# Two-layer graph network, one core: catch-up segments from block rows 12, 16, 24 on, a twelve-block tail, and three reordered steps

## What is computed

```python
def _L0(X, adj, W, b):
    deg = clip(sum(adj, axis=1) + 1.0, 1.0)
    z = concat([X, (adj @ X + X) / deg], axis=1) @ W + b
    out = relu(z);  return out / max(norm(out, axis=1), 1e-12)
def _L1(X, adj, W):
    deg = sum(adj, axis=1)
    return concat([X, adj @ X / (deg + 1.0)], axis=-1) @ W.T
x = layernorm(x + _L0(x, adj, W0, b0))
x = layernorm(x + _L1(x, adj, W1))
```

## Time and profile before

| | us |
|---|---|
| median of three runs | 753.95 (752.53 to 753.97) |
| the profiled execution, its own time | 753.86 |
| its span, first to last instruction | 751.7 |
| around the span | 2.2 |

### The profile page before, as it was taken

One profiled execution on the slowest core, in us unless ns is written; L12 is line 12 of the kernel. 1 busy time (PEld: TensorE's weight loads), 2 busy tenths in 40 slices (PEclk: granted clock), 3 DMA queues, 4 the chain that ended last, 5 costly groups with the idle time before them and its releaser, 6 DMA issues.

```text
span 751.7 us, 27897 instructions
## 1 busy us (share of the span) xinstructions
PE 632.5 (84%) x11125; PEld 579.6 (77%) x11125; DVE 670.9 (89%) x2469; ACT 618.5 (82%) x969; POOL 250.9 (33%) x344
## 2 busy tenths in 40 slices
PE   1467667778787888889899998999999999999995
PEld 0467666667676777778798887999898998989995
DVE  6879899889998998998999998999999999987894
ACT  6788898989998989899899988898998989870143
POOL 0122434333322233324335232535352434321034
PEclk9986988989999999999999999999999999999998
DMA  9999999999999999999999999999999999910002
GB/s 343 420 419 420 421 419 421 418 420 419 419 420 419 401 422 416 410 418 395 420 400 422 417 419 381 407 412 411 413 393 419 396 421 418 415 76 3 2 28 94
DMA packets 41515, 274.54 MB, mean 365 GB/s; under 512 B 4454, under 2 KB 8614, under 8 KB 8614
## 3 DMA queue, kind: packets, MB, share of 16 engines
q1 hardware_dynamic: 41152, 272.65, 88.7%
q10 hardware_dynamic: 230, 0.07, 0.0%
HBM read 270.60 MB, written 2.10 MB: 363 GB/s over the span
## 4 chain that ended last, share of the span: by engine, by line
PE 33%; DMA 23%; DVE 16%; issue 11%; ACT 10%; POOL 4%; SPq 1%; ACTq 0%; DVEq 0%; POOLq 0%
DMA a_in<-in_adj 23%; PE s_ps L388 16%; ACT junk L591 7%; PE u_ps L407 5%; DVE t_sb L812 5%; DVE e L805 4%; POOL small L1177 4%; DVE q_sb L876 2%; PE p_ps L374 2%; DVE y_sb L870 2%; PE s_ps L473 2%; PE u_ps L469 1%; PE z_ps L457 1%; PE p_ps L469 1%; SPq L339 1%
## 5 line engine op out<-in xcount | busy, mean ns | idle before, releaser
L591 ACT ACTIVATE junk<-a_in 128x2048 uint8<-128x2048 uint16 x256 | 488.6, 1912 | 17.7 <-DMA a_in<-in_adj 16.9
L388 PE MATMUL s_ps<-xh,t_sb 128*128 128x129 f16 x4096 | 389.4, 252 | 43.1 <-DVE t_sb L812 39.7
L388 PEld LDWEIGHTS s_ps<-xh,t_sb 128*128 128x128 fp8e4 x4096 | 314.3, 103 | 73.1 <-DVE t_sb L812 44.9
L805 DVE TENSOR_SCALAR e<-a_in 128x2048 uint8<-128x2048 f32 x256 | 312.0, 1225 | 24.4 <-DMA a_in<-in_adj 23.5
L1204 POOL COPY store<-pk 128x32 uint32<-128x32 uint32 (+1 forms) x250 | 151.5, 648 | 285.7 <-ACT pk L600 285.7
L812 DVE TENSOR_SCALAR t_sb<-pk 128x128 uint32<-128x128 uint32 x1024 | 156.3, 224 | 7.3 <-ACT pk L600 6.4
L374 PE MATMUL p_ps<-pow_h,e 128*128 128x16 f16 x2048 | 90.9, 171 | 66.2 <-DVE e L805 65.4
L374 PEld LDWEIGHTS p_ps<-pow_h,e 128*128 128x128 f16 x2048 | 77.8, 99 | 80.7 <-DVE e L805 68.4
L1177 POOL TENSOR_TENSOR small<-small,minus_half 128x4 f32<-128x4 f32 x32 | 70.3, 2196 | 167.9 <-DVE small L862 124.1
L407 PE MATMUL u_ps<-xh,u_sb 128*128 128x64 f16 x2976 | 105.1, 192 | 0.0
L407 PEld LDWEIGHTS u_ps<-xh,u_sb 128*128 128x128 fp8e4 x2976 | 100.1, 97 | 1.2
(11 more groups left out here) (120 smaller groups left out, 467.1 us busy)
## 6 DMA issues: line engine op xcount, KB each, us to landing
a_in<-in_adj SPq DMA_DIRECT2D x256, 1024.0 KB, 11.9
xl<-in_x SPq DMA_DIRECT2D x4, 512.0 KB, 12.8
out_h<-e SPq DMA_DIRECT2D x8, 256.0 KB, 2.5
b_sb<-in_L_gnn_b ACTq DMA_DIRECT2D x3, 0.2 KB
w_sb<-in_L_gnn_W ACTq DMA_DIRECT2D x1, 32.0 KB
w_raw<-in_L_gnn_W ACTq DMA_DIRECT2D x1, 32.0 KB
```

What stands on the lines that cost most here:

```text
L388: last = nc.tensor.matmul(s_ps[:, n % 2, at:GW], t_sb[:, b // 2, b % 2::2], xh[:, b, at:GW], start=(b == 0), stop=False)
L591: nc.scalar.activation(junk[:, t % 2, :], halves[t % R], ACT.Copy, scale=1.0 / 128, accum_out=half_sum[:, n, c:c + 1]).then_inc(s_half, 1)
L805: nc.vector.tensor_scalar(e8[:, c, :], a_in[:, t % R, :], 1.0, float(CODE), ALU.is_equal, ALU.add).then_inc(s_e, 1)
```

## The change

`START` is 0, 12, 16, 24, 32, 40, 48, 56. The column blocks below which G is known become 0, 8, 12, 20, 28, 36, 44, 52, and the widths 8, 4, 8, 8, 8, 8, 8 and 12 for the tail. The tail is two passes of six column blocks, with two matmuls of 64 columns for each block in both passes, and one addition in both. There are eight and not six tail buffers. On PE, `transpose_cat(e)` moves ahead of the fourth `pack_chunk` of its row; the wait for the last copy of sums moves behind `dense(e)` in the tail. On ACT, `take_g(e)` moves ahead of `take_packed(n, 0)`. On DVE, `low_part(e)` and `begin_acc(e)` move from the end of row k = 3 to behind the first `compare` of the next row. At the end of the tail the last group is added and squared in two halves.

```diff
-START = [0, 12, 20, 28, 36, 44, 52]
+START = [0, 12, 16, 24, 32, 40, 48, 56]
-W = 8
+LAST = 2 * NB // TG - 1
-VR = 6
+VR = 8
-WIDTH = [W] * (NQ - 1) + [NB - TAIL]
+WIDTH = [low(s + 1) - low(s) for s in range(NQ - 1)] + [NB - TAIL]
+TW = WIDTH[-1] // 2
@@ tail_sums(j) on PE
-                at = TAIL + (j // NV) * W
+                at = TAIL + (j // NV) * TW
                 for r in range(TG):
-                    for b in range(W):
-                        if j < NV:
-                            last = nc.tensor.matmul(v_ps[j % 3][:, r, :], v_sb[:, j % VR, (r * W + b) // 2, b % 2::2],
-                                                    xh[:, at + b, 0:HP], start=(b == 0), stop=(b == W - 1))
-                            continue
+                    for b in range(TW):
                         for part in range(2):
...
+                    if j == LAST and r == TG // 2 - 1:
+                        last.then_inc(s_vps, 1)
@@ PE, the loop over rows
                 for c in range(NC):
-                    pack_chunk(n, c)
                     if e >= 0 and (k, c) == (1, 3):
                         transpose_cat(e)
+                    pack_chunk(n, c)
@@ PE, the tail
-            pe.wait_ge(s_agg, NB)
             pe.wait_ge(s_uadd, NB - START[1])
+            pe.wait_ge(s_glo, (TAIL + TW + BR - 1) // BR)
             tail_sums(0)
             transpose_cat(e)
+            pe.wait_ge(s_pk, NB * 2)
             tail_sums(1)
             dense(e)
+            pe.wait_ge(s_agg, NB)
             tail_sums(2)
@@ ACT
                 sum_codes(n, 2)
-                take_packed(n, 0)
                 if e >= 0 and k == 3:
                     take_g(e)
+                take_packed(n, 0)
@@ DVE, additions of the tail
-                ins = nc.vector.tensor_tensor(rows, v_ps[j % 3][:, :, 0:F], rows, ALU.add)
-                if j < NV:
-                    link(ins)
-                    ins = nc.vector.tensor_tensor(rows, v_ps[j % 3][:, :, F:HP], rows, ALU.add)
-                ins.then_inc(s_vadd, 1)
+                nc.vector.tensor_tensor(rows, v_ps[j % 3][:, :, 0:F], rows, ALU.add).then_inc(s_vadd, 1)
@@ DVE, the loop over rows
                 compare(n, 0)
+                if e >= 1 and k == 0:
+                    low_part(e - 1)
+                    begin_acc(e - 1)
                 if n:
                     unpack(n - 1, 0)
...
-                if e >= 0 and k == 3:
-                    low_part(e)
-                    begin_acc(e)
@@ DVE, the end of the tail
             for g in range(NV):
-                if g:
+                if g == NV - 1:
+                    add_last(0)
                     variance(g - 1)
-                add_tail(NV + g)
-                if g == NV - 1:
+                    square_last(0)
+                    add_last(1)
+                    square_last(1)
                     last_variance()
+                else:
+                    if g:
+                        variance(g - 1)
+                    add_tail(NV + g)
```

More of the change, by code:

```diff
@@ L82, in piece @@
     return j * ROWS[q - 1] // steps, (j + 1) * ROWS[q - 1] // steps
-PIECE = max(piece(n)[1] - piece(n)[0] for n in range(START[1], NB))
+PIECE = max((piece(n)[1] - piece(n)[0]) * WIDTH[seg(n) - 1] for n in range(START[1], NB))
 def turn(slot):
@@ L138, in gnn_kernel @@
         store = sb("store", [P, BASE[NQ]], U32)
-        u_sb = sb("u_sb", [P, PIECE * W // 2, 2 * P], FP8)
+        u_sb = sb("u_sb", [P, PIECE // 2, 2 * P], FP8)
         xh = sb("xh", [P, NB, GW + 1], F16)
@@ L402, in catch_up @@
                         pe.wait_ge(s_uadd, turn(n))
-                half = (r1 - r0 + 1) // 2
+                half, w = (r1 - r0 + 1) // 2, WIDTH[q - 1]
                 for r in (range(half), range(half, r1 - r0))[half_of]:
-                    for b in range(W):
+                    for b in range(w):
                         for part in range(2):
-                            last = nc.tensor.matmul(u_rows[:, r, 0:F], u_sb[:, (r * W + b) // 2, b % 2::2],
+                            last = nc.tensor.matmul(u_rows[:, r, 0:F], u_sb[:, (r * w + b) // 2, b % 2::2],
                                                     xh[:, low(q - 1) + b, part * F:(part + 1) * F],
-                                                    start=(b + part == 0), stop=(b + part == W))
+                                                    start=(b + part == 0), stop=(b + part == w))
                     if r == r1 - r0 - 1:
@@ L464, in tail_sums @@
                     pe.wait_ge(s_vadd, j - 2)
-                at = TAIL + (j // NV) * W
+                at = TAIL + (j // NV) * TW
                 for r in range(TG):
-                    for b in range(W):
-                        if j < NV:
-                            last = nc.tensor.matmul(v_ps[j % 3][:, r, :], v_sb[:, j % VR, (r * W + b) // 2, b % 2::2],
-                                                    xh[:, at + b, 0:HP], start=(b == 0), stop=(b == W - 1))
-                            continue
+                    for b in range(TW):
                         for part in range(2):
-                            last = nc.tensor.matmul(v_ps[j % 3][:, r, 0:F], v_sb[:, j % VR, (r * W + b) // 2, b % 2::2],
+                            last = nc.tensor.matmul(v_ps[j % 3][:, r, 0:F], v_sb[:, j % VR, (r * TW + b) // 2, b % 2::2],
                                                     xh[:, at + b, part * F:(part + 1) * F],
-                                                    start=(b + part == 0), stop=(b + part == W))
+                                                    start=(b + part == 0), stop=(b + part == TW))
+                    if j == LAST and r == TG // 2 - 1:
+                        last.then_inc(s_vps, 1)
                 last.then_inc(s_vps, 1)
@@ L830, in unpack_piece @@
                     dve.wait_ge(s_ups, turn(n))
-                dst = words(u_sb[:, 0:(r1 - r0) * W // 2, :])
+                dst = words(u_sb[:, 0:(r1 - r0) * WIDTH[q - 1] // 2, :])
                 unpack_planes(lambda g: dst[:, :, g * 2 * PKW:(g + 1) * 2 * PKW],
@@ L924, in unpack_tail @@
                 unpack_planes(lambda t: dst[:, :, :, 2 * t * PKW:2 * (t + 1) * PKW],
-                              src[:, :, i * W // 2:(i + 1) * W // 2, :]).then_inc(s_v, 1)
+                              src[:, :, i * TW // 2:(i + 1) * TW // 2, :]).then_inc(s_v, 1)
             def add_tail(j):
@@ L932, in add_tail, with add_last, square_last @@
                 rows = acc[:, (j % NV) * TG:(j % NV + 1) * TG, :]
-                ins = nc.vector.tensor_tensor(rows, v_ps[j % 3][:, :, 0:F], rows, ALU.add)
-                if j < NV:
-                    link(ins)
-                    ins = nc.vector.tensor_tensor(rows, v_ps[j % 3][:, :, F:HP], rows, ALU.add)
-                ins.then_inc(s_vadd, 1)
+                nc.vector.tensor_tensor(rows, v_ps[j % 3][:, :, 0:F], rows, ALU.add).then_inc(s_vadd, 1)
+            def add_last(h):
+                dve.wait_ge(s_vps, LAST + h + 1)
+                dve.wait_ge(s_vadd, LAST)
+                rows = acc[:, NB - TG + h * BR:NB - TG + (h + 1) * BR, :]
+                link(nc.vector.tensor_tensor(rows, v_ps[LAST % 3][:, h * BR:(h + 1) * BR, 0:F], rows, ALU.add))
+            def square_last(h):
+                dve.wait_ge(s_fvar, NV - 4)
+                for n in range(NB - TG + h * BR, NB - TG + (h + 1) * BR):
+                    ins = nc.vector.scalar_tensor_tensor(out=sqf[:, (NV - 1) % 4, n % TG, :], in0=acc[:, n, :], scalar=1.0,
+                                                         in1=acc[:, n, :], op0=ALU.mult, op1=ALU.mult,
+                                                         accum_out=fvar[:, 1, n:n + 1])
+                link(ins)
             def variance(g):
@@ L948, in last_variance @@
                 rows = slice(NB - TG, NB)
[L949 to L955, removed]
                 nc.vector.scalar_tensor_tensor(out=fvar[:, 1, rows], in0=fvar[:, 1, rows], scalar=1.0 / F,
```

## The result

Eleven runs of each kernel gave a median of 755.49 us (754.47 to 756.72) after the change and 753.39 us (752.10 to 754.22) before it. The ratio is 1.0033, with a 95% interval of 1.0025 to 1.0042: slower by 0.33%, 2.1 us. The prediction had 751.5 us and faster as the likeliest; its range up to 757.0 holds the time.

What follows compares the result with a forecast made beforehand. Transfers with a hiccup per group of four were taken to bound rows 12 to 48, PE the rows from 44 on. Span 751.7 + 15.9 - 3.2 - 6.0 - 9.1 = 749.3, with 2.2 around it 751.5 us; range 746.5 to 757.0.

Steps and rivals of the forecast that it cites:

- The reordered steps: Rows 12 to 48: removing ACT's and DVE's waits brings PE to row 48 6.0 us sooner; bounds nothing and 12.1 us.
- g: The time by which PE reaches row 48 sooner; taken as 6.0 us, forecast range 5 to 8.
- 360 us: Rows 12 to 48: what the transfers alone want, at 420 GB/s, where the rows took 372.1 us.
- Near 420 GB/s for 35 of 40 slices: Transfer rate read from the page of the kernel before; it gave 10.0 us a block row, 40 a group of four.
- 757.5 - g: The whole kernel's time in us with the other terms kept and only the gain up to row 48 left open.
- The extra work on PE: Rows 48 to 63 and the last sums: 15.9 us more on PE, less 3.2 of its idle time, +12.7.
- The tail: From the end of the sums to the end: 9.1 us less, bounds 7.5 and 11; 63 us against 72.1 before.
- never made up: Second pass of the tail: `verdict`'s 4.2 us delay stays, as PE's pitch of 2.88 us equals the DVE loop.
- Rival 4: POOL becomes late as copies by `keep` grow from 250 to 285, under 1 us a group: 753 us, chance 0.03.
- Rival 3: Transfers become the only limit up to row 48, g 9.5 to 12, time 745.5 to 748 us; chance 0.16.
- rival 1: Rows 48 to 63: extra work hidden nowhere, reordering gives nothing, g below 2.0, 756 to 757.5 us; chance 0.22.

Runs made afterwards that it cites:

- light catch-ups: Changed kernel without the products with `g_lo` in the catch-ups of rows 48 to 63: 743.15 us in one run.
- ten steps ahead: Against segments of four, ten of `verdict`'s fifteen steps moved into two DVE waits at the head of the tail: 743.34 us.
- segments of four: Changed kernel with segments of four rows from 12 to 56, tail still twelve: 746.48 us, ratio 0.9918 against the kernel before.
- both readers lighter: Changed kernel with ACT's sums and DVE's compare doing half of each chunk from row 12 on, guard flag held at zero: 754.38 us in one run.
- a ring of five: Changed kernel with a ring of five buffers and not six, and six tail buffers and not eight: 756.1 us in one run.
- PE relieved: Changed kernel whose catch-ups of rows 12 to 47 multiply only each row's first block and its high half: 756.15 us in one run.

## Why the prediction was wrong

**The step that failed** is "The reordered steps", where it says "I take half: PE reaches row 48 by g = 6.0 us sooner". It is 1.1 us, about what two runs of the same stream differ by, and the reordering alone gives 0.9 in time. The distance to 360 us, which I took for the upper bound of a gain, was no loss through waits at all: 420 GB/s was read off single slices of the page and taken for the ceiling of a long stretch. "Near 420 GB/s for 35 of 40 slices" was itself read too kindly: 12 of the 35 in the earlier trace rows lie between 343 and 413. And the prediction did not look at DVE's wait for chunks, 12.0 us in 17 waits in the kernel before: an engine that is already waiting for data does not bring the next chunk sooner by being free sooner. Halving both readers' work, and separately leaving out three in ten of PE's matmuls, left row 48's first chunk where it was (503.8 us; 503.9 and 504.1). A wait as large as a loss need not be its cause.

The DMA share in the earlier trace rows, 1.01, is no proof of it by itself. In the changed kernel rows 52 to 55 have a share of 1.00 at 399 GB/s, and there PE sets the pace: it never idles, and DVE waits for a chunk once, for 0.3 us.

**With g = 1.1** and the rest as predicted the formula 757.5 - g gives 756.4. The extra work was 0.7 us less than predicted, the tail gave 0.2 less, and 1.8 and not 2.2 us lie around the span: 755.5, as measured.

**The extra work on PE** was right: 15.9 less 3.2 of idle time makes 12.7, measured 12.0. The groups from row 48 on take 42.1, 42.5, 45.7 and 46.2 where 42, 43, 46 and 46.5 were named, and the light catch-ups confirm that this work sets the time.

**The tail** was right: 63.2 us from the end of the sums against 63, `add_tail(8)` at 34.65 against 34.7, turns of 2.86 against 2.87. PE waits for DVE in the second pass, but only once, 0.32 us at 725.95, since the two pitches are the same (2.88 and 2.86). That `verdict` is never made up there was shown by moving it: the tail is 3.3 us shorter with ten steps ahead (59.8 against 63.1).

**Rival 4** did not come: POOL's 285 copies are hidden, and with segments of four it runs 554 instructions without a loss.

**Rival 3** was half right. The transfers were the limit up to row 48, but at 413 GB/s and already before the change. The range, which reaches 757.0 for rival 1, holds the time, but the forecast, faster with g of 5 to 8, does not. That 755.5 lies inside the range is no support for the mechanism.

## What to carry to other kernels

Before a wait of a reader is priced as a loss, look at whether the same engine also waits for its data in that stretch: here DVE did, 17 times, and removing its other waits moved the idle time to the next chunk and did little more. The DMA share does not tell (1.01 where the transfers set the pace, 1.00 where PE did); a kernel with lighter readers does. Work moved out of a tail is free only where its new place has slack, so count the blocks per group and spread them first (segments of four turned the same tail of twelve from a loss of 2 us into a gain of 6 to 7). In a tail that runs at the pitch of one engine's loop, any step in that loop's engine counts in full, and an earlier wait of the same engine is the place for it.

## What the hardware showed that was not expected

**One of the sixteen transfer streams falls behind, and DVE waits for it.** The trace has sixteen landings for each chunk (the Trainium skill, "DMA: Bandwidth & Descriptors", section "Why a DMA increments its semaphore by 16 and not by 1", says that each transfer engine reports its part; the count agrees). In the changed kernel the last of them is 0.7 us behind the first at row 0, 1.8 at row 4, 2.8 at row 12, 4.7 at row 16, 6.4 at row 24, and 5.2 to 6.9 from there to row 44; at row 36 fifteen lie within 2.6 us and one at 6.5. With both readers lighter, the last is up to 8.9 us behind; with a ring of five it is 3.2 to 4.8 from row 24 to row 44. DVE is released by the last. The last landings hardly move between the kernel before, the changed one and the one with both readers lighter: at row 24 256.8 to 256.9 us, at row 36 380.6 to 380.8, at row 48 503.7 to 503.9 (503.3 to 504.7 in all fourteen kernels). The lag stops growing, and where it stops is the larger the more buffers are free. That fits faster streams that use up the ring and then wait for the slowest, but it is inferred: the records do not name a packet's stream, so neither these waits nor whether it is always the same stream can be seen. So 36 rows take 10.3 us each, while single slices show 420 GB/s. Why one stream falls behind stays open.

**PE's instructions come over the same sixteen streams.** From 136.4 to 508.5 us the changed kernel has 43 packets of 16 KB on queue 8 and 5,509 matmuls, 128 bytes for each matmul with its weight load; with 3,844 matmuls there are 30, again 128 bytes each. (The Trainium skill, "Runtime: NRT & Kernel Launch", section "Instruction fetch mechanics", has 16 KiB blocks that the sequencer fetches itself, mostly hidden; the size agrees.) Where such a packet ends, the records show a data packet that starts there and takes long, where the median of the 8 KB ones is 0.311 us:

```
start us   queue  bytes  us
58.90      8      16384  1.076
59.96      1       8192  0.804
84.98      8      16384  1.098
86.06      1       8192  0.774
111.85     14      8192  0.324
112.16     1       8192  0.968
```

In that stretch a packet of queue 8 takes 0.9 to 1.2 us and one of queue 14 0.31 to 0.55, with up to 0.97 for the data packet behind it. That this is what throws the slowest stream back was the natural story, and for queue 8 the run with PE relieved speaks against it: 13 of 43 packets are gone, and row 48's first chunk lands at 504.1 us and not sooner. Spread evenly, though, 13 x 1.08 / 16 = 0.9 us a stream would be an estimate of their worth, and single runs cannot show that much. For queue 14, which has 22 to 24 packets there in the kernels looked at, it was not tried.
